# A windowed-attention block whose six gelu tiles get buffers of their own, with every engine's pieces in a new order

## The reference

```
xl = layernorm(x over channels); roll by (-3, -3); cut into 7 x 7 windows of 49 tokens
q, k, v = split(xw @ qkv_w.T + qkv_b), 6 heads of 32
attn = softmax(q @ k.T * 32**-0.5)
out = (attn @ v) @ proj_w.T + proj_b; windows put back; roll by (3, 3)
xl = layernorm(out); h = gelu(xl @ fc1_w.T + fc1_b)          # 768 hidden channels
return (h @ fc2_w.T + fc2_b) as channels first + x           # x is the shortcut
```

## Time and profile before

| what | value |
|---|---|
| time, median of 3 runs | 3117.31 us (3116.3 to 3117.31) |
| the profiled execution | 3117.07 us, span 3115.2 us |
| mean granted clock of TensorE | 0.996 of full |
| TensorE busy | 3078.9 us, 28076 instructions |
| ScalarE busy | 2709.6 us, 5502 |
| VectorE busy | 2490.3 us, 7339 |
| GpSimd busy | 936.4 us, 1292 |
| transfers | 129.33 MB, mean 42 GB/s |

### The profile page before, as it was taken

One profiled execution on the slowest core, in us unless ns is written; L12 is line 12 of the kernel. 1 busy time (PEld: TensorE's weight loads), 2 busy tenths in 40 slices (PEclk: granted clock), 3 DMA queues, 4 the chain that ended last, 5 costly groups with the idle time before them and its releaser, 6 DMA issues.

```text
span 3115.2 us, 77363 instructions
## 1 busy us (share of the span) xinstructions
PE 3078.9 (99%) x28076; PEld 2991.3 (96%) x28076; DVE 2490.3 (80%) x7339; ACT 2709.6 (87%) x5502; POOL 936.4 (30%) x1292
## 2 busy tenths in 40 slices
PE   6999999999999999999999999999999999999998
PEld 5999999999999999999999999999999999999998
DVE  6788788878888887788788878887888888878876
ACT  3988888888888888888888888888888888888887
POOL 1223322332233233323322332233223323332332
PEclk8999999999999999999999999999999999999999
DMA  3121112111221221122112211211221122112211
GB/s 69 31 45 43 39 40 45 42 38 41 43 43 39 42 47 39 39 44 44 38 40 44 44 38 40 46 41 39 41 47 39 38 42 47 39 39 44 44 29 28
DMA packets 458711, 129.33 MB, mean 42 GB/s; under 512 B 392803, under 2 KB 458084, under 8 KB 458340
## 3 DMA queue, kind: packets, MB, share of 16 engines
q1 hardware_dynamic: 455012, 122.71, 18.7%
q10 hardware_dynamic: 3328, 1.68, 0.2%
HBM read 47.20 MB, written 38.54 MB: 28 GB/s over the span
## 4 chain that ended last, share of the span: by engine, by line
PE 98%; SPq 1%; DVE 1%; ACT 0%; issue 0%; POOL 0%; DMA 0%; POOLq 0%; DVEq 0%; ACTq 0%
PE psum L311 8%; PE psum L313 7%; PE psum L312 7%; PE psum L314 7%; PE psum L315 7%; PE psum L593 6%; PE psum L568 6%; PE psum L548 5%; PE psum L549 4%; PE psum L559 4%; PE psum L550 4%; PE psum L560 4%; PE psum L574 4%; PE psum L518 4%; PE psum L321 3%; PE psum L323 3%
## 5 line engine op out<-in xcount | busy, mean ns | idle before, releaser
L926 DVE BATCH_NORM_STATS2 st<-psum 98x6 f32<-98x192 f32 x1024 | 354.7, 357 | 223.6 <-PE psum L495 223.5
L745 ACT ACTIVATE hh<-psum,b 128x392 fp32r<-128x392 f32 x768 | 451.5, 588 | 43.8 <-PE psum L315 29.2
L1133 POOL TENSOR_TENSOR ve<-mv,eps 98x4 f32<-98x4 f32 x256 | 80.1, 313 | 1290.2 <-DVE mv L932 1290.2
L748 ACT ACTIVATE hf<-psum,b 128x392 f32<-128x392 f32 x768 | 447.4, 583 | 0.0
L937 DVE TENSOR_SCALAR xn<-psum,mv,rs 98x192 f32<-98x192 f32 x1024 | 422.5, 466 | 6.3 <-POOL rs L1135 6.3
L977 DVE TENSOR_TENSOR hl<-hf,hh 128x392 fp32r<-128x392 f32 x640 | 350.6, 548 | 10.3 <-ACT hf L748 6.2
L1147 POOL TENSOR_TENSOR pr<-pr,rc 98x294 f32<-98x294 f32 x512 | 338.9, 681 | 17.6 <-DVE rc L1013 17.6
L708 ACT ACTIVATE pt<-psum 113x294 f32<-113x294 f32 x512 | 213.4, 417 | 125.1 <-PE psum L574 107.0
L548 PE MATMUL psum<-hh,w2h 128*128 128x392 f32 x768 | 286.4, 373 | 0.0
L311 PE MATMUL psum<-x_h,w_mh 128*128 128x392 f32 x768 | 281.1, 366 | 0.0
L1152 POOL TENSOR_TENSOR xt<-yr,xt 64x392 f32<-64x392 f32 x128 | 131.0, 1024 | 458.3 <-DVE yr L990 458.3
(11 more groups left out here) (137 smaller groups left out, 9980.7 us busy)
## 6 DMA issues: line engine op xcount, KB each, us to landing
vbd<-vs SPq DMA_DIRECT2D x1024, 36.8 KB
xt<-in_x SPq DMA_DIRECT2D x112, 194.5 KB, 2.7
out<-xt SPq DMA_DIRECT2D x112, 194.5 KB, 2.0
xt<-in_x SPq DMA_DIRECT2D x112, 97.2 KB, 2.4
out<-xt SPq DMA_DIRECT2D x112, 97.2 KB, 2.1
xt<-in_x SPq DMA_DIRECT2D x112, 48.2 KB, 2.2
xt<-in_x SPq DMA_DIRECT2D x256, 0.8 KB, 2.0
xt<-in_x SPq DMA_DIRECT2D x128, 1.5 KB, 2.2
```

The source lines that it names most:

```text
L745: nc.scalar.activation(hh[:, m % HB, :], bank("fc1", m)[:, 0:T], ACT.Gelu, bias=b1[:, m:m + 1]).then_inc(s_hh, 1)
L748: nc.scalar.activation(hf[:, m % HB, :], bank("fc1", m)[:, 0:T], ACT.Gelu, bias=b1[:, m:m + 1]).then_inc(s_gelu, 1)
```

## The change

`HB` becomes `MT`, so that each of the six hidden tiles has a buffer of its own in `hf`, `hh` and `hl`. `gelu_hi` waits for the last layer's matmuls of the same tile in the unit before, for all six tiles. `BANK_USES` is a new table, `LAGS` is 6 where it was 5, SyncE's loop stores unit t - 4 where it stored t - 3, and every engine's `step` has its pieces in another order and partly with other lags. No piece is added or taken away.

```diff
-HB = 3
+HB = MT
...
-BANK_USES = [("o", 0, 5, 3), ("o", 1, 7, 3), ("fc1", 0, 4, 4), ("vt", 1, 0, 2), ("fc1", 1, 1, 4),
...
+BANK_USES = [("qkv", 3, 2, 2), ("fc1", 2, 7, 5), ("qkv", 2, 1, 2), ("fc1", 3, 3, 5), ("vt", 1, 4, 2),
+             ("fc1", 4, 2, 5), ("fc1", 5, 0, 5), ("pt", 0, 7, 3), ("x1", 0, 6, 1), ("pt", 1, 3, 3),
...
-LAGS = 5
+LAGS = 6
...
-            for t in range(UNITS + 3):
+            for t in range(UNITS + 4):
...
-                u = t - 3
+                u = t - 4
...
             def gelu_hi(u, m):
                 if u == 0 and m == 0:
                     act.wait_ge(s_bias, 3)
-                if m >= HB:
-
-                    act.wait_ge(s_pe["fc2"], nth(u, MT, m - HB))
-
+                if u > 0:
+
+                    act.wait_ge(s_pe["fc2"], nth(u - 1, MT, m))
```

More of the change, by code:

```diff
@@ L613, in step @@
                 u = units(t)
-                if u[3] is not None:
+                if u[2] is not None:
+                    qkv(u[2], 3)
+                if u[5] is not None:
+                    fc1(u[5], 2)
+                if u[2] is not None:
+                    qkv(u[2], 2)
+                if u[5] is not None:
+                    fc1(u[5], 3)
+                if u[2] is not None:
+                    values(u[2], 2)
+                    values(u[2], 3)
+                if u[5] is not None:
+                    fc1(u[5], 4)
+                    fc1(u[5], 5)
+                if u[3] is not None:
+                    probs_t(u[3], 0)
+                if u[1] is not None:
+                    x1_channels(u[1], 0)
+                if u[3] is not None:
+                    probs_t(u[3], 1)
+                if u[2] is not None:
+                    scores(u[2], 0)
+                if u[3] is not None:
+                    probs_t(u[3], 2)
+                if u[4] is not None:
+                    x2_channels(u[4], 0)
+                if u[2] is not None:
+                    scores(u[2], 1)
+                    scores(u[2], 2)
+                if u[1] is not None:
+                    x1_channels(u[1], 1)
+                if u[3] is not None:
+                    probs_t(u[3], 3)
                     weighted(u[3], 0)
@@ L618, in step @@
                     weighted(u[3], 3)
+                if u[0] is not None:
+                    to_tokens(u[0], k, it, 0)
+                if u[4] is not None:
+                    x2_channels(u[4], 1)
+                if u[0] is not None:
+                    to_tokens(u[0], k, it, 1)
+                if u[2] is not None:
+                    scores(u[2], 3)
+                if u[5] is not None:
+                    fc2_hi(u[5], 0)
+                    fc2_hi(u[5], 1)
+                    fc2_hi(u[5], 2)
+                    fc2_lo(u[5], 0)
+                    fc2_hi(u[5], 3)
@@ L619, in step @@
+                if u[1] is not None:
+                    qkv(u[1], 4)
+                    values(u[1], 0)
+                    values(u[1], 1)
+                if u[5] is not None:
+                    fc2_hi(u[5], 4)
+                    fc2_hi(u[5], 5)
                 if u[4] is not None:
                     fc1(u[4], 0)
[L621 to L623 removed]
+                if u[5] is not None:
+                    fc2_lo(u[5], 1)
@@ L624, in step @@
+                if u[3] is not None:
+                    project(u[3], 0)
+                if u[5] is not None:
+                    fc2_lo(u[5], 2)
+                if u[3] is not None:
+                    project(u[3], 1)
+                    project(u[3], 2)
+                    project(u[3], 3)
                 if u[4] is not None:
                     fc1(u[4], 1)
[L626 to L630, removed]
@@ L645, in step @@
[L645 to L663, removed]
@@ L679, in step @@
[L679 to L687, removed]
+                if u[5] is not None:
+                    fc2_lo(u[5], 3)
+                    fc2_lo(u[5], 4)
+                    fc2_lo(u[5], 5)
             steps(step)
@@ L850, in step @@
                 if u[0] is not None:
-                    hi_part("x1", u[0], 1)
+                    q_out(u[0], 0)
                 if u[3] is not None:
                     gelu_full(u[3], 2)
-                if u[1] is not None:
-                    exps(u[1], 0)
+                    gelu_hi(u[3], 3)
+                    gelu_full(u[3], 3)
             steps(step)
```

246 lines of the change are left out of this document (117 added, 129 removed), and 11 rows, old and new, of the table BANK_USES.

## The result

The changed kernel takes 3108.74 us (median of 16 runs, 3104.37 to 3114.39) where the kernel before takes 3116.65 beside it (16 runs, 3115.2 to 3117.63): ratio 0.9975, interval 0.9968 to 0.9983. It gained 7.9 us where 17 were forecast. It lies inside the range and on the forecast side. A second thing stands out in the times: the runs of before lie 2.4 us apart, those of after 10.

A forecast was written before the change was run, and what follows sets the result against it. TensorE's sequence and its switches between plain and wide blocks were taken to bound the kernel. 3117.07 - 17.9 for switches + 0.5 for draining gave 3099.7, 3099.9 against the median: 3100 us, range 3092 to 3113.

The forecast's parts named there:

- What bounds it: Whole kernel: TensorE's sequence sets the 23.865 us step, with no wait in it that a deeper buffer could remove.
- The gelu buffers worth nothing: Hidden tiles: six gelu buffers by themselves gain nothing, since the matmuls into them never wait for a gelu tile.
- The switches: TensorE's plain-wide changes: cost falls from 0.39 to 0.24 us per unit; 0.14 taken as saved, 17.9 us in all.
- Entry: Going from probability transposes into the weighted block on TensorE: costs 0.10 us, before and after.
- Exit: Leaving the weighted block on TensorE: 0.20 us before, 0.11 after, with a transpose of x behind it.
- Scores 3 into the last layer: TensorE's switch from scores 3 to the last layer's wide matmuls: costs 0.03 us, bounded by 0 and 0.03.
- Case 2: Rival at the weighted block's exit: 0.20 us whatever follows, saving only 0.06 per unit, 7.7 us, giving 3110; chance 0.15.
- TensorE stays fed: Steady steps in the new order: other engines and transfers keep up, so waits cost nothing.
- ScalarE's cover: Bank 2, passing from fc1 4 to scores 1: gelu_full 4 ends 0.44 us before scores 1 want it.
- The 0.8: Transfers from vs to vbd: v_out 0 ends at 20.1 us, 0.8 before project 2 wants bank 5.
- case 4: Rival: late vbd transfers stall v_out 0 and TensorE once per unit, 38 us less the 17.9, giving 3138; chance 0.10.
- Filling and draining: Start and end of the run: filling taken as 0, between -3 and +8 us; draining costs 0.5 us.

The follow-up runs named there:

- e2: The kernel before with six gelu buffers and the new gelu_hi wait alone, its order kept: 3111.91 us, ratio 0.9986.
- e8: The kernel before with hf, hh and hl allocated for six tiles, three used, no instruction or wait changed: 3110.81 us, ratio 0.9982.
- e9: The kernel before with an unused tile laid behind hl, the three hidden tiles staying in place: 3116.24 us, ratio 0.9999.
- e10: The kernel before with an unused tile laid ahead of hf, moving everything from hf on together: 3116.41 us, ratio 1.0001.
- e4: e1 with the weighted block cut into two halves and scores 3 between them: 3133.8 us, ratio 1.0056 to the kernel before.
- e1: The changed kernel with two buffers for vs, so v_out waits for the transfers of unit u - 2: 3094.26 us, ratio 0.993.

## Why the prediction was right or wrong

**What bounds it: right.** TensorE's sequence sets the step, and from 110 to 3060 us TensorE waits for nothing but the one row above.

**The gelu buffers worth nothing: wrong.** No wait goes away, as argued, but their size moves `hh` and `hl`, and that is worth 4.5 us (e2) or 5.5 us (e8). No term of the sum was there for it. e9 and e10 exclude what lies behind and a common shift; whether distance or place counts is open.

**The switches: the mechanism right, the exit mis-sized.** This is the run of plain work in the changed kernel, to be read against the earlier trace rows:

```profile
1506.00 0.42 PE L574 MATMUL psum<-ident,pr 98*128 98x98 f32 x3
1506.35 1.61 PE L593 MATMUL psum<-pt,vbd 113*64 113x49 f32 x48
1507.88 0.42 PE L493 MATMUL psum<-ident,xt 128*98 128x128 f32 x2
1508.14 0.27 PE L495 MATMUL psum<-ident,xt 128*98 128x128 f32 x1
...
1508.42 0.38 PE L493 MATMUL psum<-ident,xt 128*98 128x128 f32 x2
1508.64 0.27 PE L495 MATMUL psum<-ident,xt 128*98 128x128 f32 x1
1508.75 0.51 PE L568 MATMUL psum<-km,qm 128*98 128x98 f32 x4
...
1509.21 0.43 PE L548 MATMUL psum<-hh,w2h 128*128 128x392 f32 x1
1509.48 0.34 PE L549 MATMUL psum<-hh,w2l 128*128 128x392 f32 x1
```

- Entry: three transposes take 0.35 (1506.00 to 1506.35) against 0.25, so 0.10, as forecast.
- Exit: the block is again 1.53 long, a tail of 0.09 as before, and the two transposes behind it take 0.26 (1507.88 to 1508.14) where the second pair takes 0.22 (1508.42 to 1508.64). 0.09 + 0.04 = 0.13, against 0.11 taken and 0.20 before.
- Scores 3 into the last layer: 1508.75 to 1509.48 is 0.73, against 0.52 + 0.18 = 0.70: 0.03, as forecast.

So the sum after is 0.26, not 0.24, and the switches save 0.13 us per unit: 0.39 - 0.26. The step shows 23.865 - 23.70 = 0.165, and the tiles' places give 0.03 to 0.05 of it (e2 and e8; that they give as much in the new order is assumed), which leaves 0.12 to 0.13. Both ways agree. A forecast of 0.14 was right in size; its neighbour, the 0.03, was missing. In all, 128 x 0.165 = 21.1 us were saved, against 17.9.

Case 2, that the exit stays at 0.20, falls for the changed order; the exit depends on what follows the block, 0.13 to a transpose and 0.19 to scores (e4). The rule of the Trainium skill, "TensorEngine Tiling (Array Packing)", section Tiling Modes (Key Properties), that a change of tiling mode drains TensorE, is borne out in kind: every border of the block costs, and adding two of them costs 0.26 us per step (e4). It gives no price, and one price for all exits would have been wrong. That this block writes 64 partitions, which I gave as its mark, isn't enough: L560 writes 64 too, between wide matmuls, and the next one starts 0.18 us behind it as behind other wide ones (changed kernel):

```profile
730.95 0.34 PE L560 MATMUL psum<-hl,w2h 128*64 128x392 f32 x1
731.13 0.25 PE L321 MATMUL psum<-wp_mh,o_h 128*98 128x192 f32 x1
```

By the kernel's text the weighted block alone writes partitions 64 to 127 by themselves; whether that is what costs, no run here shows.

**TensorE stays fed: here the prediction failed.** The step was: "So I cost the waits of the steady part at nothing, with these covers: 0.44 on ScalarE, 0.8 on the vbd transfers." ScalarE's cover held. The 0.8 was wrong twice. First, its size: the transfers end 0.3 later than 5.8 + 2.0, and from the start of the copy to TensorE's next block are 733.31 - 732.61 = 0.70 us, where I had put the copy's 0.55 and no hand-over. Together 0.4 is left. That alone would have cost nothing, since an ordinary unit fits in it. Second, a cover was held against one duration, the usual one. The transfers are now and then 1.3 us later, and then TensorE stands. This is the mechanism of case 4 with its place and its queue, but in some units only: 8.4 us in the profiled execution, where case 4 had 38 for every unit. My own row of evidence showed the spread: "762/777/869" are the issues of one stretch, and over the whole span of the changed kernel the longest is twice the median (duration in ns, min/median/max):

```profile
L416 SPq DMA_DIRECT2D vbd<-vs x1024: 762/778/1691, 41.7 to 3058.2; - x171
```

Not every late unit has a slow issue; the one above has eight ordinary ones. What makes those transfers late isn't shown, but the kept traces say where to look, at the transfers of the kind instruction in the page's third section (packets, MB, share):

```profile
q8 instruction: 233, 3.82, 0.5%
q14 instruction: 142, 1.16, 0.1%
```

In the eleven traces of this case 78 of 11000 issues into `vbd` took over 0.9 us, and each of the 78 had one of these in flight, where 17% of all issues had one. In 48 of 1364 units the packets of the last issue ended more than 1.95 us behind its start (usual: 1.85), and again all 48 had one in flight, where 22% of the units had. Each of the eleven long steps of the changed kernel has such an issue or such a landing. Most issues and units with one in flight weren't late, and no run changes these transfers, so this is a coincidence without exception and not a cause shown.

My layout of the step also has a small slip: by its own prices the last wide block ends at 3.60 + 0.89 + 1.80 = 6.29, not 6.36. It shifts what follows and changes the covers by less than 0.1.

**Filling and draining: right in sum once the transfers are out of the way, in part by luck.** e1 has 3093.0 - 128 x 23.70 = 59.4 us beside its steps, the kernel before 60.5. But the clock was kinder to e1: granted 0.75 and 1.00 from 40 to 60 and 60 to 80 us, where the kernel before had 0.64 and 0.83. That is up to 5.6 us that no term of the prediction had, so the extra step may have cost something that the clock gave back. In the changed kernel the filling has 4.7 us more, mostly by the same wait: in the first units, where TensorE has little else, `v_out` stands 2.85 and 2.50 us for transfers. The prediction had put -3 to +8 here and taken 0; the cause it named (probabilities in one plain run) isn't what was seen.

**The sum.** 3116.65 - 21.1 for the steps is 3095.5, less 1.1 for a filling that is slightly shorter is 3094.4; e1 measured 3094.26. The late transfers give back 3108.74 - 3094.26 = 14.5 us of the median. The forecast of 3100 missed the kernel with the late transfers by 8.7 and is 5.7 above the one without them. The switches alone, 128 x 0.13 = 16.6 us against the 17.9 taken, were right; the 5.7 are about what the tiles' places give, which it didn't have.

## What to carry to other kernels

Hold a cover behind a transfer against the latest of its landings, not against the usual one, and count the hand-overs on both sides; where it is thin, double the tile on one side of the chain before trusting it, since the copy of 3 KB per partition here is worth 14.5 us and nothing in the order before. A scatter of runs that grows with a change (here from 2.4 to 10 us, and back to 1.3 without the wait) is a sign to look for such a wait. And when a change alters the size of a buffer, run the old kernel with only the room changed: part of the difference may be where the tiles lie.

## What the runs showed of the hardware

- Issues of SyncE for the same transfer took 0.78 us usually and up to 1.69, and with eight ordinary issues the landing was once 1.32 us later than one step before. In eleven traces all 78 issues over 0.9 us and all 48 late landings coincided with a transfer of the kind instruction; the cause isn't shown.
- The price of leaving the block of 64-partition products depends on the successor: 0.20 to a wide matmul, 0.19 to scores, 0.13 to a transpose; entering it costs 0.09 to 0.10.
- Where the tiles of the hidden layer lie in memory moved a whole kernel by 5.5 us (e8, ratio 0.9982, interval 0.9974 to 0.9991), with no instruction changed, while moving them together (e10) or what lies behind them (e9) left the time as it was. Moving them together did change the spacing of single matmuls, from 180.1 to 176.0 ns in one group. The cause is open.
